# A gated state-space layer with a quantised MLP on one Trainium2 core: h turned by DMA, a second bank for a, states added on GpSimd, more products on VectorE

## What is computed

```python
# state-space layer: dt, B, C, u from the second input; 16 states n per channel
def step(state, inp):
    d, b, c, u = inp
    state = state * jnp.exp(d[..., None] * A) + (d * u)[..., None] * b[:, None, :]
    return state, jnp.einsum('bdn,bn->bd', state, c)
y = (scan(step) + D * u) * silu(layernorm(x))
x = x + tanh(g_xattn) * y
# MLP: bitlinear = rmsnorm, round to 8 bits per row, times ternary weights
h = silu(bitlinear(layernorm(x), w1)) * bitlinear(layernorm(x), w2)   # 2048 wide
x = x + tanh(g_ffn) * bitlinear(h, w3)
```

## Time and profile before

| | us |
|---|---|
| median of 3 runs | 655.52 |
| lowest, highest | 654.02, 656.09 |
| profiled execution | 653.69 |
| its span | 651.9 |

### The profile page before, as it was taken

How to read it: one execution, slowest core, us unless ns; L and a number is a source line. 1 busy time by engine, 2 the same in 40 slices (tenths; PEclk the granted TensorE clock), 3 DMA queues, 4 the chain that set the end, 5 groups by cost and what they waited for, 6 DMA issues and landing times.

```text
span 651.9 us, 7928 instructions
## 1 busy us (share of the span) xinstructions
PE 488.3 (75%) x2560; PEld 296.4 (45%) x2560; DVE 583.0 (89%) x772; ACT 530.7 (81%) x969; POOL 587.9 (90%) x289
## 2 busy tenths in 40 slices
PE   8798878994564678777666486778676887668987
PEld 3254434552553445455534354455454554345543
DVE  6779779997998899999999999989997999999765
ACT  5764767788999778987798797899999898897675
POOL 1399999998999999999999999999999999999431
PEclk9988999997555979999786889889989897978999
DMA  5598587579960100147420100037700000000001
GB/s 186 193 407 309 183 329 276 198 270 389 374 262 0 39 1 2 47 153 276 132 78 0 33 2 17 1 127 244 254 37 1 17 1 18 0 16 18 1 17 48
DMA packets 24472, 80.77 MB, mean 124 GB/s; under 512 B 2464, under 2 KB 5152, under 8 KB 21360
## 3 DMA queue, kind: packets, MB, share of 16 engines
q1 hardware_dynamic: 24432, 80.27, 33.9%
HBM read 72.53 MB, written 7.73 MB: 123 GB/s over the span
## 4 chain that ended last, share of the span: by engine, by line
POOL 30%; DVE 29%; ACT 14%; issue 13%; PE 11%; DMA 2%; SPq 0%; DVEq 0%; POOLq 0%; ACTq 0%
POOL hh L708 15%; POOL hh L818 14%; DVE hh L773 9%; DVE hh L770 8%; DVE room L1048 4%; ACT da L736 3%; DVE sm L1093 2%; PE bank_a L1020 2%; PE bank_b L1029 2%; PE bank_y L851 2%; ACT room L1041 1%; PE da L1211 1%; DVE bank_y L576 1%; DVE sm L904 1%; ACT gbuf L922 1%
## 5 line engine op out<-in xcount | busy, mean ns | idle before, releaser
L773 DVE TENSOR_TENSOR_SCAN hh<-da,hh 128x1024 f32<-128x1024 f32 x85 | 193.4, 2280 | 3.1 <-ACT da L743 3.0
L851 PE MATMUL bank_y<-ident,hh 128*128 128x128 f32 x1024 | 145.3, 292 | 10.8 <-POOL hh L818 8.8
L851 PEld LDWEIGHTS bank_y<-ident,hh 128*128 128x128 f32 x1024 | 129.6, 152 | 40.1 <-issue 17.5
L813 POOL TENSOR_TENSOR hh<-hh,cc 128x1024 f32<-128x1024 f32 x60 | 141.0, 2350 | 0.2 <-ACT hl L756 0.2
L818 POOL TENSOR_TENSOR hh<-hh,cc 128x1024 f32<-128x1024 f32 x57 | 134.2, 2355 | 0.0
L708 POOL TENSOR_TENSOR hh<-pair,bb 128x1024 f32<-128x1024 f32 x30 | 70.5, 2352 | 26.4 <-DMA bb<-xd_scratch 24.2
L770 DVE TENSOR_TENSOR_SCAN hh<-da,hl,hh 128x256 f32<-128x256 f32 x128 | 85.4, 729 | 0.0
L708 POOL TENSOR_TENSOR hh<-wq,bb 128x1024 f32<-128x1024 f32 x32 | 75.3, 2357 | 1.8 <-PE bank_y L851 1.8
L702 POOL TENSOR_TENSOR hh<-wq,bb 128x1024 f32<-128x1024 f32 x32 | 75.1, 2346 | 0.3 <-PE bank_y L851 0.3
L702 POOL TENSOR_TENSOR hh<-pair,bb 128x1024 f32<-128x1024 f32 x32 | 75.2, 2355 | 0.0
L736 ACT ACTIVATE da<-wq,cst 128x256 f32<-128x256 f32 x128 | 53.3, 463 | 12.0 <-DVE hh L770 11.6
(11 more groups left out here) (271 smaller groups left out, 1051.7 us busy)
## 6 DMA issues: line engine op xcount, KB each, us to landing
bb<-xd_scratch SPq DMA_DIRECT2D x32, 512.0 KB, 5.1
cc<-xd_scratch SPq DMA_DIRECT2D x32, 512.0 KB, 6.9
wq<-weights SPq DMA_DIRECT2D x12, 1024.0 KB, 6.5
stage<-weights SPq DMA_DIRECT2D x8, 1024.0 KB, 6.1
xin<-x SPq DMA_DIRECT2D x4, 1024.0 KB, 5.4
room<-weights SPq DMA_DIRECT2D x4, 1024.0 KB, 8.2
u_scratch<-wq SPq DMA_DIRECT2D x6, 512.0 KB, 3.0
wq<-x SPq DMA_DIRECT2D x2, 1024.0 KB, 18.8
```

Source lines behind the costliest of these rows:

```text
L773: ins = v.tensor_tensor_scan(to, da, h, 0.0, ALU.mult, ALU.add)
L813: ins = g_.tensor_tensor(quarters(flat(hh[k % NH])), quarters(flat(hh[k % NH])), cc[:, n:n + 4, t], ALU.mult)
L851: mm = pe.matmul(bank_y[:, (first + c) * P:(first + c + 1) * P], flat(hh[k % NH])[:, at:at + P], ident[:, :], start=False, stop=(s == STEP ...
```

## The change

1. **h turned by DMA** (tiles 0 to 11, `by_dma`). `ht_tensor` and `hqt_scalar` go; SP issues two DMA transposes per tile in slot 8, each of 128x1024 fp16, when the half is rounded. The offset of 1536 stays in; one matmul with one row, -1536 times the column sums of w3, opens the product. The column sums are made once in slot 36, by 16 matmuls and one eviction, and the turn of tile 0's x waits for them.
2. **Two banks for a.** Odd chunks of a go to `bank_t`. So `out_tensor` also waits for the last gated chunk of the next tile.
3. **States of first halves are added on GpSimd.** Scans of second halves are one instruction from 0. Before each, GpSimd adds the kept state, times exp(dt a) of the half's first position (`state_gain` on ScalarE, `carried` on GpSimd), to the first element of each state (`add_state`).
4. **One-piece peaks and squares** of 2048, and a shorter chain of small operations: VectorE three per tile, ScalarE two (`rk_scalar`, `fin_scalar`). The power on GpSimd moves from slot 7 to slot 6 of a tile; VectorE's scale waits for `rk_scalar`.
5. **Seven more products by C on VectorE**: steps 47, 59, 79, 85, 97, 109 and 121.

Cut to its core:

```diff
-BY_VECTOR = (14, 16, 25, 45, 49, 53, 62, 67, 68, 73, 77)
+BY_VECTOR = (14, 16, 25, 45, 47, 49, 53, 59, 62, 67, 68, 73, 77, 79, 85, 97, 109, 121)
...
+        def column_sums(pe):
+            pe.wait_ge(*WA.of(("sign", NW - 1)))
+            pe.wait_ge(*YV.of(("p", NE - 1)))
+            pe.wait_ge(*PV.of("ident16"))
+            for f in range(KF):
+                mm = pe.matmul(bank_t[0:1, :], ones16[:, :], w3q[:, f, :], start=(f == 0), stop=(f == KF - 1))
+            WP.did(mm, "columns")
+        def column_sums_scalar(act):
+            act.wait_ge(*WP.of("columns"))
+            WA.did(act.activation(w3sum, bank_t[0:1, :], ACT.Copy), "columns")
...
+        def carried(g_, k):
+            b, h, q, n = where_split(k)
+            if n == 0:
+                g_.wait_ge(*HA.of(("gain", b)))
+                g_.wait_ge(*HA.of(PER * b + 4 * q + 3))
+                HG.did(g_.tensor_tensor(hl[:, q, :], hl[:, q, :], gain[:, q, :], ALU.mult), ("carried", k))
+        def add_state(g_, k):
+            b, h, q, n = where_split(k)
+            g_.wait_ge(*HG.of(("product", k)))
+            first = quarters(flat(hh[k % NH]))[:, :, 0]
+            g_.tensor_tensor(first, first, hl[:, q, n:n + 4], ALU.add).then_inc(s_m1, 1)
...
+        def state_gain(act, b):
...
+            for q in range(NE):
+                g = NE * b + 2 + q // 2
+                ins = act.activation(gain[:, q, :], a_neg[:, q, :], ACT.Exp,
+                                     scale=dt2[g % 4][:, HALF * (q % 2):HALF * (q % 2) + 1])
...
-            if split(k) and where_split(k)[1]:
-                b, _, q, n = where_split(k)
-                for j in range(4):
-                    t = slice(HALF * j, HALF * (j + 1))
-                    ins = v.tensor_tensor_scan(to[:, t], da[:, t], h[:, t], hl[:, q, n + j:n + j + 1],
-                                               ALU.mult, ALU.add)
-            else:
-                ins = v.tensor_tensor_scan(to, da, h, 0.0, ALU.mult, ALU.add)
-            ins.then_inc(s_scan, 1)
+            v.tensor_tensor_scan(to, da, h, 0.0, ALU.mult, ALU.add).then_inc(s_scan, 1)
...
+            if by_dma(i) and c % 2:
+                return bank_t, bank_b
...
+        def square_scalar(act, i):
+            act.wait_ge(*MV.of(("h", i, NCH - 1)))
+            MA.did(act.activation(view(room, 4096, 1024).bitcast(BF16), h_all(i), ACT.Square,
+                                  accum_out=ssq[:, 0:1]), ("sq", i))
...
+        def rk_scalar(act, i):
+            act.wait_ge(*MG.of(("rh", i)))
+            MA.did(act.activation(rk, rh, ACT.Copy, scale=kk[:, i % NE:i % NE + 1]), ("rk", i))
+        def scale_vector(v, i):
+            v.wait_ge(*MV.of(("peak", i)))
+            v.wait_ge(*MA.of(("rk", i)))
+            MV.did(v.tensor_scalar(hm, am1, rk, 1e-5, ALU.mult, ALU.max), ("hm", i))
+            v.wait_ge(*MV.now())
+            MV.did(v.reciprocal(hinv, hm))
+            v.wait_ge(*MV.now())
+            MV.did(v.tensor_scalar(csh, hinv, rk, 127.0, ALU.mult, ALU.mult), ("csh", i))
...
+        def turn_by_dma(sp, i):
+            for r in range(2):
+                sp.wait_ge(*MA.of(("hq", i, r)))
+                if r == 0 and i:
+                    sp.wait_ge(*MP.of(("o", i - 1)))
+                d_turn[r].did(sp.dma_start_transpose(hqT16[:, 8 * r:8 * r + 8, :], h16_at(i, r)), ("hqT", i, r))
...
+            if by_dma(i) and 0 in groups:
+                pe.wait_ge(*ZA.of(("gT", max(j for j in range(NE, 4 * NE) if z_turn_slot(j) < turned(i) + 2))))
+                if tile_slot(i + 1) - 1 < turned(i) + 2:
+                    pe.wait_ge(*MA.of(("xqT", i + 1)))
+                    if by_dma(i + 1):
+                        pe.wait_ge(*MV.of(("g", i + 1, NCH - 1)))
+                pe.wait_ge(*WV.of("offset"))
+                pe.matmul(bank_g(i)[:, :], offset, w3sum, start=True, stop=False)
```

More of the change, by code:

```diff
@@ L37 @@
 TOTAL = 19
+SUMS = 36
 PAIR = {2: 25, 3: 37, 4: 49, 5: 64, 6: 87, 7: 99}
@@ L174, in build @@
         gates = cst[:, 92:94]
-        col = iter(range(282))
+        col = iter(range(285))
         def small(n=1):
@@ L193, in build @@
         ssq, ssv, amh = [small(3) for _ in range(3)]
-        am1, ram1, rh, rk_most, rk_am, csh = [small() for _ in range(6)]
+        am1, ram1, rh, rk, rk_most, rk_am, hm, hinv, csh = [small() for _ in range(9)]
         fin = [small() for _ in range(2)]
@@ L221, in build @@
         hl = sb("hl", [P, NE, NS])
+        gain = ones[:, 0:NE * NS].rearrange("p (e n) -> p e n", e=NE)
         heads = sb("heads", [P, GN])
@@ L643, in weight_mean @@
             WV.did(v.reciprocal(winv, wmean))
+            WV.did(v.memset(offset, -MAGIC16), "offset")
             v.wait_ge(*PA.of("gates"))
@@ L704, in times_b @@
                                            [P, 4, HALF]), bb[:, n:n + 4, t], ALU.mult)
+                if h:
+                    HG.did(ins, ("product", k))
+                    return
             else:
@@ L1001, in chunk_before, with a_before @@
             return (i, c - 1) if c else (i - 1, NCH - 1)
+        def a_before(i, c):
+            if by_dma(i):
+                return (i, c - 2) if c >= 2 else (i - 1, 2) if c == 0 else None
+            return chunk_before(i, c)
         def a_tensor(pe, i, c):
-            a, before = bank_ab(i, c)[0], chunk_before(i, c)
+            a, before = bank_ab(i, c)[0], a_before(i, c)
+            if by_dma(i) and c == 1:
+                j = max(j for j in range(NE, 4 * NE) if z_turn_slot(j) < tile_slot(i) + 1)
+                pe.wait_ge(*ZA.of(("gT", j)))
             if c == 0:
@@ L1014, in a_tensor @@
                 pe.wait_ge(s_scan, ALL - 1)
-            if before[0] >= 0 and at_end(before[0]):
+            if before is not None and before[0] >= 0 and at_end(before[0]):
                 pe.wait_ge(*MA.of(("th", *before)))
-            elif before[0] >= 0:
+            elif before is not None and before[0] >= 0:
                 pe.wait_ge(*MV.of(("g", *before)))
@@ L1368, in _ @@
                     for i in range(END - 1):
+                        if k == turned(i):
+                            turn_by_dma(sp, i)
                         if k == turned(i) + 3:
@@ L1555, in _ @@
                                 rows_scalar(act, END, 1)
+                    for b in SPLIT:
+                        if k == PAIR[2 * b + 1] + 1:
+                            state_gain(act, b)
                 for k in range(80, SLOTS):
@@ L1563, in _ @@
                             tanh_scalar(act, i, c)
+                    if c_by_vector(k + LEAD - 2):
+                        keep_state(act, k + LEAD - 2)
                     if k + LEAD < ALL:
                         exp(act, k + LEAD)
-                    if k + LEAD - 2 < ALL:
+                    if k + LEAD - 2 < ALL and not c_by_vector(k + LEAD - 2):
                         keep_state(act, k + LEAD - 2)
@@ L1590, in _ @@
                     for i in range(END):
-                        if k == tile_slot(i) + 2 or k == tile_slot(i) + 4:
-                            square_scalar(act, i, k - tile_slot(i) - 1)
+                        if k == tile_slot(i) + 4:
+                            square_scalar(act, i)
+                    for i in range(END):
+                        if k == tile_slot(i) + 6:
+                            rk_scalar(act, i)
                     for i in TILES:
@@ L1692, in _ @@
                     for i in range(END - 1):
-                        if k == tile_slot(i) + 9:
-                            ht_tensor(pe, i, 1)
-                    for i in range(END - 1):
                         if k == tile_slot(i) + 10:
@@ L1700, in _ @@
                             z_turn_tensor(pe, i)
-                    for i in range(END - 1):
-                        if k == tile_slot(i) + 8:
-                            ht_tensor(pe, i, 0)
                     for n in PAIR:
@@ L1884, in _ @@
                             rows_vector(v, first, n)
-                    for i in range(END):
-                        if k == tile_slot(i) + 5:
-                            scales_vector(v, i, 0)
                     for first, n, done in TURNS:
@@ L1906, in _ @@
                             du_vector(v, 2 * n + 1)
-                    for i in range(END):
-                        if k == tile_slot(i) + 2:
-                            peak_vector(v, i, 0)
                 for k in range(80, SLOTS):
@@ L1935, in _ @@
                         if k == tile_slot(i) + 4:
-                            peak_vector(v, i, 1)
-                    for i in range(END):
-                        if k == tile_slot(i) + 2:
-                            peak_vector(v, i, 0)
+                            peak_vector(v, i)
                     for i in range(END - 1):
```

146 lines of the change are left out of this document (75 added, 71 removed).

## The result

The changed kernel takes 663.23 us (median of 4 runs, 661.89 to 665.95) against 655.63 us for the kernel before: ratio 1.0125, 95% interval 1.0089 to 1.0162, so 7.6 us slower. Forecast were 651.4 us and, most likely, a gain. The profiled execution has a span of 659.9 us against 651.9.

A forecast was written before the change was run, and what follows sets the result against it. The prediction took GpSimd as the bound, VectorE next. Its terms, -6.4 (GpSimd) + 1.3 (TensorE waits) + 1.0 (column sums) = -4.1 us, turned 653.69 into 649.6, median 651.4 us; range 642 to 664 us.

The forecast's parts named there:

- GpSimd sets the pace and VectorE is the next bound: Main stretch, about 30 to 605 us: lasts as long as GpSimd has work; VectorE 2.8 us ahead at step 94.
- The sign that the prediction had named for being wrong: In the changed profile: GpSimd waiting for TensorE's sums in many tiles; other signs were named beside it.
- GpSimd: -6.4 us: GpSimd's work: seven products by C leave (-16.4 us), 40 small operations at 0.25 us come (+10.0 us).
- VectorE: -11.4 us, "can follow": VectorE's work: shorter scans, peaks and chain against seven added products, net -11.4 us, so it keeps up with GpSimd.
- Column sums: 1.0 us taken, 0 to 3 us named: Slot 36: column sums of w3 delay the sums GpSimd wants at 210.90 us; 0 to 3 us late, 1.0 taken.
- New waits of TensorE: 1.3 us: w3's product, sharing a bank, waits for the next tile's gated chunk 3; 2.3 us late in tile 8, 1.3 lost in all.
- Two banks for a: nothing: Much of TensorE's 49.1 us wait for the bank of a goes; at most a few tenths per tile, costed at nothing.
- DMA transposes: 3 us each, hidden: Turning h in tiles 0 to 11: two transfers at 3 us each fit in the 9.5 us before w3's product.
- Rival 4: Turned h arrives late if a pair exceeds 10.5 us; at 20 us a pair, 765 us; chance 0.07.
- Power a slot earlier, peaks and squares: nothing: GpSimd's earlier power, with a one-piece square, might make it wait 1 to 2 us; costed with the rest at nothing.
- Rival 1: VectorE and handoffs take the gain, so the 6.4 us shrink to nothing: 654 to 657 us; chance 0.19.
- Rival 3: Small GpSimd operations are dear, 0.54 us each: +7.5 us with the waits for sums, 663 us; chance 0.15.

The follow-up runs named there:

- e7: Kernel before with all of the change except turning h by DMA, the column sums and the second bank for a; 660.1 us, ratio 1.0078.
- e4: Changed kernel with the seven products by C given back to GpSimd; 665.7 us, ratio 1.0160 to the kernel before.
- e5: Kernel before with only first-half states added on GpSimd, one-piece second-half scans and seven more products by C on VectorE; 659.5 us, ratio 1.0082.
- e6: Kernel before with only the longer table, seven more products by C on VectorE; 663.5 us, ratio 1.0140.
- e9: e5 with the product of step 91 given to VectorE in place of step 97; 656.2 us, ratio 1.0023 to the kernel before.
- e3: Changed kernel without column sums (part of the result missing) and with one bank for a; 658.2 us, ratio 1.0056 to the kernel before.
- e8: Kernel before with only one-piece peaks and squares, the shorter small-operation chain and the power a slot earlier; 655.7 us, ratio 1.0010.
- e10: e5 with VectorE's added products only in second halves (85, 90, 91, 115, 120, 121); 653.3 us, ratio 0.9984 to the kernel before.
- e11: e7 with the table of e10; 653.0 us, ratio 0.9971 to the kernel before.
- e12: Changed kernel with one bank for a, column sums in slots 45 and 46, and the table of e10; 653.1 us, ratio 0.9982 to the kernel before.

## Why the prediction was wrong

**"GpSimd sets the pace and VectorE is the next bound": this step failed.** It rested on GpSimd without idle time and on step 94, where the scan ended 2.8 us before the product by C began. That showed only that GpSimd was late for VectorE's output. The other direction was in the same trace and was not read:

```profile
438.64 2.35 POOL L702 TENSOR_TENSOR hh<-wq,bb 128x1024 f32<-128x1024 f32 x1
...
449.38 2.67 DVE L770 TENSOR_TENSOR_SCAN hh<-da,hl,hh 128x256 f32<-128x256 f32 x4
```

This is the kernel before, step 94: GpSimd's product by B ends at 441.0 and VectorE's scan of it starts at 449.4, 8.4 us late. Between steps 45 and 126 no scan starts less than 1.7 us behind its product by B; half of them are over 5.6 us behind. Each engine was late for the other, so both were full. VectorE's 49.1 of 50 us said so too. The 2.8 us were not room that VectorE had; they were a stock between two full engines. The sum priced this part at -6.4 us; e7, which has it and neither the turn by DMA nor the second bank, is 5.1 us slower than the kernel before. That is 11.5 of the 11.8 us by which the forecast missed. The sign that the prediction had named for being wrong, GpSimd waiting for sums in many tiles, is there (17.1 us, 14 times).

**GpSimd: -6.4 us.** Measured 8.4 us less work of its own (40 small operations cost 8.0 us, forecast 10.0; 7 x 2.35 as forecast); its busy time fell by 9.5, because the records of neighbouring instructions overlap by some 0.05 us. Size right, worth in time wrong: 2.5 us for the seven products (e4), less than nothing for the trade (e5).

**VectorE: -11.4 us, "can follow".** Its busy time fell by 10.7 us, so the sum was right. It was made over the whole run, though, while the scans get shorter only in second halves. Elsewhere VectorE only gained work, at 1.23 us a product (47, 59, 79, 97, 109). The text noted this unevenness and priced it at nothing; it also said that three of the seven fall before step 64, where it is two. By e6 such a product costs its 1.25 us in full, and step 97 more, 3.9 us in e6 and 3.3 us when e9 moved it to 91; 1.9 of that (in e6 and in e5 alike) was a wait for the row of C, which the prediction did not look for.

**Column sums: 1.0 us taken, 0 to 3 us named.** They cost 3.2 to 3.7 us. The end of the matmuls (207.8 us) lay inside the range given. But only the sums behind them were followed, to GpSimd. GpSimd's wait there was 1.0 us, as forecast. The cost went by ScalarE and VectorE (5.2 us idle), and VectorE, itself a bound, could not make it good.

**New waits of TensorE: 1.3 us.** The mechanism was the one forecast, seen in tile 7 with 2.5 us. Its size was missed in two ways: the longer pauses lower the clock for the product behind them (four take 5.2 to 5.3 us where in the kernel before one does, 50.1 us for the twelve products instead of 45.0), and nine products wait, not one. Yet only 1.4 to 1.8 us reach the end, near the noise and near the 1.3 us taken.

**Two banks for a: nothing.** Right for the gain: the wait moved from a to b, whose bank was not doubled.

**DMA transposes: 3 us each, hidden.** Right: 3.2 us, and w3's product waits for the chunk nine times, once for ScalarE (2.4 us) and never for a DMA; by e3 against e7 if anything a small gain. The Trainium skill, "VectorE: DVE Perf Modes" (The three transpose paths), gives 1309 ns for a 128x128 block by DMA. Eight blocks in one transfer land here in 3.2 us, 0.4 us a block, so the estimate of 10.5 us that the prediction made from that figure does not hold for this form; how long one block by itself takes no run shows. Rival 4 falls.

**Power a slot earlier, peaks and squares: nothing.** Right (e8, within 0.25%).

**Rivals.** Rival 1 named the mechanism, but let the gain shrink "to nothing" (654 to 657 us) where it turned into a loss. Rival 3 reached 663 us by a cause that was not there: the small operations cost 0.20 us, not 0.54. The range, 642 to 664, holds the time only because of rival 3: that is luck.

## What to carry to other kernels

Before moving work from one full engine to another, measure the lateness between them in both directions: if each starts late on what the other has long finished, both are the bound, and a trade can only pay where the receiver has lost work in the same stretch. Make the balance by stretch, not over the run; e9 and e10 won 3.3 and 6.2 us over e5 by changing numbers in a table. Expect less than the sum even so: e10 got 1.4 of 6 us over the kernel before. A new wait on an engine with slack is priced by following everything queued behind it on every engine, with the clock at which the engine comes back.

## What was not expected of the hardware

A wait of 2.5 us in front of w3's product brought TensorE from a granted clock of 1.00 (476 to 483 us) to 0.54 (483.3 to 487 us), nearly all of it at the 1.2 GHz level, and sixteen matmuls from 3.6 to 5.3 us; in the kernel before the same tile's product follows other matmuls at once, at 1.00.

A DMA transpose of 128x1024 two-byte elements on the chip took 3.2 us (median of 24, the longest 5.2), less than the 5.5 us of a plain load in the earlier trace rows. It is not free for its neighbours: with the 24 of them the run has 49815 packets instead of 24472, over half of them under 512 B, and the loads of B and C land later. In e7 and then in e3, which has the transposes besides:

```profile
bb<-xd_scratch SPq DMA_DIRECT2D x32, 512.0 KB, 4.9
cc<-xd_scratch SPq DMA_DIRECT2D x32, 512.0 KB, 6.6
...
bb<-xd_scratch SPq DMA_DIRECT2D x32, 512.0 KB, 5.6
cc<-xd_scratch SPq DMA_DIRECT2D x32, 512.0 KB, 7.3
```

From e11 to e12 they go from 5.2 to 6.0 and from 7.0 to 8.2 us. In the six kernels with transposes the median for C is 7.3 to 8.2 us, in the eight without 6.6 to 7.2. Each is one profiled execution, and by e3 against e7 no time is lost by it.
